# GpSimd waits for VectorE's norm application before it takes up the scatters and the split parts

## The reference, cut to what matters

```python
x = _layernorm(x + block(x, ...), axis=-1)      # (x - mean) / sqrt(var + 1e-5)
```

## Time and profile before

| | us |
|---|---|
| median of 3 runs (lowest, highest) | 1496.15 (1493.22, 1500.85) |
| the profiled execution, its own time | 1497.72 |
| its span from first to last instruction | 1496.0 |
| TensorE busy | 1135.4 (76%) |
| VectorE busy | 952.6 (64%) |
| ScalarE busy | 614.8 (41%) |
| GpSimd busy | 486.2 (32%) |

### The profile page before, as it was taken

One profiled execution on the slowest core, in us unless ns is written; L12 is line 12 of the kernel. 1 busy time (PEld: TensorE's weight loads), 2 busy tenths in 40 slices (PEclk: granted clock), 3 DMA queues, 4 the chain that ended last, 5 costly groups with the idle time before them and its releaser, 6 DMA issues.

```text
span 1496.0 us, 32177 instructions
## 1 busy us (share of the span) xinstructions
PE 1135.4 (76%) x9171; PEld 822.8 (55%) x9171; DVE 952.6 (64%) x3478; ACT 614.8 (41%) x1352; POOL 486.2 (32%) x695
## 2 busy tenths in 40 slices
PE   2799899889199994776728998999976899337950
PEld 1355555554188883664516776777654566225730
DVE  3688888886423324996836776777557687761237
ACT  1266556656044441335403554555554232113410
POOL 6112433434535453233441111111024111352553
PEclk9599889989599996997657999999977797558985
DMA  4655445531367767211025443444010000133523
GB/s 118 72 59 62 70 67 76 69 59 40 115 196 201 207 198 228 74 43 32 18 31 70 53 53 48 52 55 47 17 29 28 22 25 11 44 110 92 167 78 91
DMA packets 152567, 117.02 MB, mean 78 GB/s; under 512 B 16001, under 2 KB 140674, under 8 KB 152322
## 3 DMA queue, kind: packets, MB, share of 16 engines
q1 hardware_dynamic: 145282, 101.18, 34.2%
q0 software_dynamic: 7168, 14.37, 2.9%
HBM read 47.26 MB, written 23.41 MB: 47 GB/s over the span
## 4 chain that ended last, share of the span: by engine, by line
PE 46%; DVE 23%; issue 10%; DMA 7%; POOL 6%; SPq 3%; ACT 3%; DVEq 1%; POOLq 0%; ACTq 0%
PE po L1485 7%; PE po L431 6%; DVE xg L334 4%; PE pt L1479 4%; DVE mx L601 4%; PE pm L1479 3%; SPq L367 3%; PE pt L391 2%; PE pt L394 2%; PE pm L412 2%; DMA xs<-xg 2%; POOL rstd L327 2%; PE pm L417 2%; PE pm L418 2%; PE p L522 2%
## 5 line engine op out<-in xcount | busy, mean ns | idle before, releaser
L601 DVE TENSOR_REDUCE mx<-pm 128x2 f32<-128x512 f32 (+1 forms) x512 | 306.3, 619 | 163.2 <-PE pm L418 97.8
L553 ACT ACTIVATE ex<-pt 128x512 f32<-128x512 f32 (+1 forms) x512 | 271.1, 544 | 207.9 <-PE pt L391 99.3
L324 POOL TENSOR_SCALAR ve<-mv 128x2 f32<-128x2 f32 x96 | 25.5, 266 | 560.6 <-DVE mv L318 560.6
L1562 POOL DMA_INDIRECT result<-ye,to_row x128 | 122.9, 960 | 151.3 <-issue 107.2
L431 PE MATMUL po<-ex,va 128*32 128x256 f32 (+1 forms) x2048 | 157.7, 381 | 5.2 <-ACT ob L562 5.2
L412 PE MATMUL pm<-ks,qs 96*128 96x256 bf16 x512 | 110.7, 303 | 11.5 <-DVE mx L601 10.9
L308 ACT COPY xt<-p 128x256 f32<-128x256 f32 x112 | 41.8, 373 | 175.1 <-PE p L304 175.1
L1485 PE MATMUL po<-he,we 128*128 128x256 f32 (+1 forms) x448 | 112.9, 395 | 0.6 <-DVE yt L1523 0.4
L334 DVE TENSOR_SCALAR xg<-res,mv,rstd 128x128 f32<-128x128 f32 (+1 forms) x192 | 90.1, 536 | 32.6 <-POOL rstd L327 32.6
L391 PE MATMUL pt<-qs,ks 99*128 99x256 bf16 x512 | 105.7, 292 | 6.4 <-DMA qs<-mt 3.1
L303 PE MATMUL p<-ident,xs 128*128 128x128 f32 x112 | 40.4, 361 | 85.2 <-DMA xs<-xg 81.9
(11 more groups left out here) (281 smaller groups left out, 2788.5 us busy)
## 6 DMA issues: line engine op xcount, KB each, us to landing
we<-in_pack SPq DMA_DIRECT2D x40, 514.5 KB
xs<-xg SPq DMA_DIRECT2D x112, 128.0 KB, 2.2
qs<-parts SPq DMA_DIRECT2D x192, 64.0 KB
ks<-parts SPq DMA_DIRECT2D x192, 64.0 KB
we<-in_pack SPq DMA_DIRECT2D x16, 512.0 KB
xe<-sorted SPq DMA_DIRECT2D x56, 132.0 KB, 2.2
yr<-result SPq DMA_DIRECT2D x48, 128.0 KB, 2.2
xr<-xg SPq DMA_DIRECT2D x32, 128.0 KB, 4.8
```

The lines of the kernel that those rows point to most:

```text
L553: nc.scalar.activation(ex[j % 2][:, 2 * u:2 * u + 2, lo:S], pt[:, u, :].rearrange("p (b k) -> p b k", k=S)[:, :, lo:S], ACT.Exp).then_inc( ...
L601: nc.vector.tensor_reduce(mx[q.slot % 2][:, qt, 4 * b + 2 * u:4 * b + 2 * u + 2], pm[:, u, :].rearrange("p (b k) -> p b k", k=S)[:, :, 0:h ...
L1562: pool.indirect_dma_start(out=rows, out_offset=bass.IndirectOffsetOnAxis(ap=to_row[q.slot][0:m, i:i + 1], axis=0), in_=ye[q.slot][0:m, i, ...
```

## The change

One line is added to the step of `heads_pool`. Having worked out `rstd` for the sequence at lag 5, GpSimd waits until `ln_x` shows that VectorE has applied it, which is two increments for every sequence so far. The line stands in the shared function, so it holds for layer 0 (`n = 0`) and layer 2 (`n = 48`). It applies in each step that has a sequence at lag 5: sixteen steps in each stage.

```diff
             def step(at):
                 if (q := at(5)):
                     norm_rstd(pool, q, n)
+                    wait_apart(pool, ln_x, 2 * (n + q.n + 1), passed)
                 if routed and (q := at(8)):
                     wait_apart(pool, place_sb, q.n + 1, passed)
                     number(pool, q, 0, xr[q.slot][:, :, :, D:D + 1])
```

## The result

The changed kernel takes 1536.74 us (median of 4 runs, 1531.37 to 1543.73) against 1498.5 for the kernel before in the same comparison (4 runs, 1493.22 to 1502.25). The ratio is 1.0264, 95% interval [1.0225, 1.0304]: slower by 2.6%. The prediction had the sign and layer 0's path right, but 1536.74 lies outside its range of 1507 to 1531, and layer 2's loss came by a path that it had dismissed. The loss is 38.2 us where 23.9 were forecast. The execution that the profiler took is the fastest of the four, 1531.37 us with a span of 1529.6.

A forecast was written before the change was run, and what follows sets the result against it. VectorE's pair, held by GpSimd's `rem`, was on the chain of waits, but layer 0's logits would come later. Terms 16.6 + 4.4 + 0.7 + 2.2 = +23.9 us gave 1521.6, 1520 as median; range 1507 to 1531.

The forecast's parts named there:

- the sign: Whole kernel: the change makes it slower, by 23.9 us; chance of slower 0.81.
- The pair: VectorE's two norm instructions at line 334: from 1.97 us in layer 0 and 1.33 in layer 2 to 0.60.
- Layer 0, the path to the logits: Eight steps with norm, scatter and parts: TensorE's logits come 2.07 us later in the mean, 16.6 us in all.
- The clock: Layer 0's eight steps: TensorE's longer stalls lower its granted clock, costing 4.4 us, bounds 0 and 9.
- The transfers: Rival: stacking transfers and `xr` come late too, adding up to 13.6 us, 1534 us; chance 0.08.
- line 580 and `ob`: Layer 2, eleven steps: `ob` starts 0.2 us later behind line 580 and two exponentials, 2.2 us, bounds -5.5 and +5.
- The last step and the early ones: Layer 0: numbering starts 0.7 us later in the last step; three early steps count 0, bounds -1.7 and +1.5.
- The rivals: Three: VectorE's gain comes through, 1475 us (0.08); no change, about 1499 (0.11); stacking transfers late too, 1534 (0.08).
- VectorE's 19 us: Rival, both layers: the shortened pairs count in full, -20.7 us with three early steps, 1475 us; chance 0.08.

The follow-up runs named there:

- writes late: Kernel before, without the wait, in layer 0 with the numbering and all four indirect writes moved behind the two parts and `xb`: 1490.96 us, ratio 0.9955.

## Why the prediction was wrong

**The pair: right.** 0.59 and 0.60 us, as forecast.

**Layer 0, the path to the logits: right in kind, too small.** From the pair's start to line 502 I summed 6.41 us; this step has 6.78 (203.49 to 210.27), the mean of eight 6.89. The hand-over to the numbering took 0.88 for 0.80, numbering to remainder 3.44 for 3.45; what I left out are the five rank matmuls ahead of the logits (lines 1299 to 1303, 209.96 to 210.27). Against the norm's start the logits come at 11.0 us; in the seven profiles in which GpSimd doesn't wait in layer 0, at GpSimd's order of before and the pair in its place, they come at 8.38 in the mean: 2.63 a step and 21.0 for eight, where the sum had 2.07 and 16.6. This term was mis-sized by 4.4 us.

**The clock: about right.** The eight steps take 168.0 us in the mean of those seven profiles (164.5 to 172.0) and 192.9 in the three with the wait (191.1 to 194.8): +24.9. The logits' 21.0 leave 3.9 for the clock and the rest, 4.4 forecast. The clock went from 0.92 in the mean to 0.86, and TensorE stood still for 3.8 us in each step (30.4 over eight). Clock and rest were not measured apart. The clock also differs among the seven, from 0.87 (171.8 us) to 0.98 (164.9); by these two, 0.06 of it would be worth some 3.8 us, an estimate.

**The transfers: dismissed too lightly in both layers.** I gave them 0.08 as something that comes on top. In layer 0 they are instead one of two rings under the logits' (the other is the exponentials behind line 580, which the sum counted for `ob` in layer 2 alone), and add nothing that shows while the logits are later. In layer 2 they are the step that failed most. I followed the later parts to line 580 and `ob` and took 0.2 us a step; I did not follow them past SyncE to what shares the DMA engines with them. The twelve transfers start 1.0 us later against the norm, the two small ones of `mt` do not, and stand behind them. The term was 2.2 us; it measured 6.7 in the traces (205.1 us in the mean of the six without the wait in the table, 211.8 in that of the four with it) and 9.4 in the medians. The stalls for the rows account for some 3.7 of it; the remainder of the gap stays open.

**The last step and the early ones: right, as far as can be told.** From GpSimd's norm in the last step to its last write it takes 24.9 us after and 24.1 before, +0.8 for the +0.7 forecast. The three early steps take 55.2 to 61.5 us without the wait and 56.1 to 61.2 with it.

**The sum.** Between 1520 and 1536.7 lie, by the medians of the two runs with the wait in one layer, 6.8 us of layer 0 (28.5 against a forecast 21.7), 7.2 of layer 2 (9.4 against 2.2), and 2.35 by which the kernel before measured more in this comparison (1498.5) than in the first (1496.15): 16.4 of 16.7. By the traces they are 3.9 and 4.5, and the other 6 us I can't place: the profiled execution of after lies 5.4 us under its median.

**The rivals.** VectorE's 19 us came through nowhere in full. The Trainium skill's rule (SBUF — State Buffer, "Who interferes with whom") is that issue order decides which of the two engines is held. The trace agrees in layer 2, where the pair begins 0.17 us behind the remainder and ends 0.34 behind it. In layer 0 of the kernel before it doesn't, by the recorded starts: VectorE's first instruction begins at 199.34, 0.47 us ahead of the remainder, and takes 1.72 us, where it takes 0.34 after the change, while the remainder keeps its 1.17.

## What to carry to other kernels

A wait costs what stands behind it in the engine's queue. Here an idle time of 3.9 us in each step went with 25 us in the eight steps where the numbering and two writes stood between it and the remainder, and with no loss against the kernel before where the remainder stood directly behind it; so put the instruction that others wait for first, before arguing over the wait. And when a producer of transfers moves, follow not only its own consumers but also the small transfers that share the DMA engines with it, which may be just in time.

## What the runs showed that I had not expected

The two-instruction pair was not made longer by GpSimd's indirect write: beside one of 0.96 us, which ran from 217.29 to 218.25, it took 0.59 us (217.81 to 218.40), though its first instruction took 0.46 there in place of 0.34. Beside the remainder it took 1.33 to 1.98, unless it began only at the remainder's end: in the kernel before with writes late it begins at 174.73, 0.27 us before the remainder ends, and takes 0.60. The two transfers for `mt`'s rows took 6.2 us from issue to use behind a backlog. And single profiles of one and the same stretch without the wait differ by 7.5 us (164.5 to 172.0), the two longest at the lowest clocks (0.87 and 0.88), so that the 169.8 of the kernel before was no safe base for a term of 2 us a step.
